# Attention layers: one program per engine for both halves, last block first, and the maxima split in four operations

## The reference

```python
x = x + _L0_xattn_ref(_layernorm(x), ctx_1024, mask_BxS2_bk0, ...)      # L0x: q and k normalised per head
x = x + _L0_attn_ref(_layernorm(x), ...)                                # L0a: self attention, j >= i
x = x + _L0_ffn_ref(_layernorm(x), ...)                                 # L0f: 8 experts, top 2
x = x + _L1_xattn_ref(_layernorm(x), ctx_1024, ctx_1024, mask, ...)     # L1x: mask per query and key
x = x + _L1_attn_ref(_layernorm(x), ...)                                # L1a: a window of 64 keys
x = x + _L1_ffn_ref(_layernorm(x), ...)                                 # L1f: 8 experts, top 2
```

## Time and profile before

| | |
|---|---|
| three runs | 1831.36, 1822.53, 1828.62 us (median 1828.62) |
| the profiled run | 1820.44 us, span of the core 1818.6 us |
| PE busy | 1631.3 us, 90% of the span |
| DVE busy | 1036.0 us, 57% |
| ACT busy | 530.2 us, 29% |
| POOL busy | 98.4 us, 5% |
| mean granted clock of PE | 0.949 of full |

### The profile page before, as it was taken

The page is one execution under the profiler, slowest core; times in us unless marked ns, Lnnn a source line. Parts: engine busy times, 40 slices in busy tenths (PEclk is TensorE's granted clock), DMA queues, the critical chain, the costliest instruction groups (busy, mean ns, idle before and its releaser), DMA issues. The chain is left out here.

```text
span 1818.6 us, 27921 instructions
## 1 busy us (share of the span) xinstructions
PE 1631.3 (90%) x9406; PEld 750.2 (41%) x9407; DVE 1036.0 (57%) x1695; ACT 530.2 (29%) x780; POOL 98.4 (5%) x82
## 2 busy tenths in 40 slices
PE   4899997999888979999999799997999788969997
PEld 1333333222233356665665233322222234467775
DVE  3577776999745541111111589996799734643223
ACT  1343423788412401111111111113588512300000
POOL 0100000200001010000001200002000001010001
PEclk9999988999989989999999799988999998979999
DMA  3424443311044749666661413315221020048996
GB/s 137 161 69 170 163 156 102 94 48 46 0 129 101 90 201 342 228 243 229 230 236 45 132 59 115 110 52 184 66 70 46 1 81 30 2 168 317 330 325 210
DMA packets 80244, 250.95 MB, mean 138 GB/s; under 512 B 7744, under 2 KB 25168, under 8 KB 60208
## 3 DMA queue, kind: packets, MB, share of 16 engines
q1 hardware_dynamic: 71568, 230.97, 38.1%
q10 hardware_dynamic: 6048, 10.69, 1.6%
q0 software_dynamic: 2560, 8.39, 1.4%
HBM read 222.50 MB, written 38.01 MB: 143 GB/s over the span
## 5 line engine op out<-in xcount | busy, mean ns | idle before, releaser
L1429 ACT ACTIVATE BIG<-banks 128x1024 f32<-128x1024 f32 (+5 forms) x320 | 282.1, 933 | 120.0 <-PE banks L1364 119.9
L993 DVE CUSTOM_DVE_ANT_0 BIG<-banks,MASK,MX 128x512 bf16<-128x512 f32 (+5 forms) x384 | 229.4, 656 | 68.2 <-issue 38.3
L1882 PE MATMUL banks<-KF,BIG 128*128 128x160 f32 (+1 forms) x1792 | 230.3, 289 | 5.0 <-DVE KF L1638 1.9
L1882 PEld LDWEIGHTS banks<-KF,BIG 128*128 128x128 f32 x1792 | 227.2, 191 | 17.2 <-issue 15.2
L654 PE MATMUL banks<-KF,XN 32*128 32x512 f32 (+4 forms) x1280 | 200.3, 633 | 16.6 <-DVE MX L993 7.7
L1904 PE MATMUL banks<-BIG,PB 128*128 128x512 f32 x448 | 202.8, 600 | 0.0
L1361 PE MATMUL banks<-XN,KF 32*128 32x512 f32 (+4 forms) x1280 | 173.3, 611 | 22.8 <-ACT BIG L1429 7.8
L1479 DVE TENSOR_TENSOR PB<-PB,BIG 128x2048 f32<-128x2048 f32 (+5 forms) x78 | 164.8, 2113 | 33.3 <-ACT BIG L1429 28.8
L986 DVE TENSOR_REDUCE MXW<-banks 128x2 f32<-128x1024 f32 x128 | 150.4, 1217 | 50.9 <-PE banks L665 49.8
L629 PE MATMUL banks<-WV,XNT 128*128 128x512 f32 x320 | 162.2, 628 | 0.0
L1331 PE MATMUL banks<-BIG,V 128*32 128x512 f32 (+4 forms) x1280 | 159.4, 568 | 3.2 <-ACT BIG L1429 2.8
(11 more groups left out here) (278 smaller groups left out, 1450.2 us busy)
## 6 DMA issues: line engine op xcount, KB each, us to landing
BIG<-in_L0f_w SPq DMA_DIRECT2D x64, 1024.0 KB, 4.7
BIG<-in_L1f_w SPq DMA_DIRECT2D x48, 1024.0 KB, 5.3
BIG<-in_mask_q SPq DMA_DIRECT2D x16, 1024.0 KB, 9.2
CT<-in_ctx SPq DMA_DIRECT2D x9, 1024.0 KB, 4.8
XNT<-in_ctx SPq DMA_DIRECT2D x8, 1024.0 KB, 5.9
k_saved<-KF SPq DMA_DIRECT2D x32, 256.0 KB, 2.6
v_saved<-V SPq DMA_DIRECT2D x32, 256.0 KB, 2.4
KF<-k_saved SPq DMA_DIRECT2D x32, 256.0 KB, 3.4
```

What stands on the lines that cost most here:

```text
L993: last = v.tensor_tensor_reduce(m.JUNK[:, 2 * half + e, k0:k1], pair[:, e, k0:k1], bias, 1.0, mx, ALU.add, ALU.max, mx)
L1429: a.activation(m.PE_[:, s % NP, 2 * half:2 * half + 2, q0:q1], m.pair[(2 * s + half) % 3][:, :, q0:q1], ACT.Exp).then_inc(exp_ready, 1)
L1882: last = t.matmul(out, W1[k][:, d, f * P:(f + 1) * P], XE[:, d, :], start=d == 0, stop=d == DC - 1)
```

## The change

`row_maxima` and `weighted_values` no longer open a program each. Both return the parts of the five engines, and `attention` opens one program in which an engine runs its part of the first half and then of the second. The semaphores of both halves are raised before it, with one barrier.

```diff
 def attention(nc, m, L, weights):
-    row_maxima(nc, m, L)
-    weighted_values(nc, m, L, weights)
+    A = row_maxima(nc, m, L)
+    first, second = A.parts, weighted_values(nc, m, L, weights, A)
+    raise_all(nc, m)
+    with nc.Block() as block:
+        @block.sync
+        def _(sp):
+            second.sync(sp, first.sync(sp))
...
```

```diff
-                with sp.If(i + 1 >= nb):
-                    for kb in range(KT_):
-                        keep_values(i, kb)
...
             if dyn:
-                load_mask(0)
-                for c in range(DC):
-                    load_keys(0, c)
-
-                for sem in m.past:
-                    wait_alone(sp, sem, nb * 16 + 16 + B)
+                if L.row_mask:
+                    wait_alone(sp, A.bias_ready, nb + A.B)
+                    load_mask(nb)
+                wait_alone(sp, A.context_loaded, nb * 16 + 16 + A.B)
+                wait_alone(sp, A.v_projected, nb * KT_ + A.B)
+            else:
+                sp.wait_ge(A.v_projected, KT_)
             O.load_output_weights(sp)
...
-                        load_keys(i + 1, c)
+                        load_keys(i, c)
```

```diff
-            v.tensor_scalar(R, m.MX[:, :], -1.0, None, ALU.mult).then_inc(steps_done, 1)
-            dve.wait_ge(cleared, 2)
-            k = 1
-            for j in range(3):
-                dve.wait_ge(steps_done, k)
-                v.tensor_copy(PART[:, :], R).then_inc(steps_done, 1)
-                dve.wait_ge(steps_done, k + 1)
-                v.tensor_copy(parts[:, :, j], PART[:, :]).then_inc(steps_done, 1)
-                v.tensor_tensor(R, R, PART[:, :], ALU.subtract).then_inc(steps_done, 1)
-                k += 3
...
+            dve.wait_ge(A.slots_zeroed, 2)
+            v.tensor_scalar(parts[:, :, 0], m.MX[:, :], -1.0, None, ALU.mult).then_inc(steps_done, 1)
+            dve.wait_ge(steps_done, 1)
+            v.scalar_tensor_tensor(R, m.MX[:, :], -1.0, parts[:, :, 0], ALU.mult, ALU.subtract).then_inc(steps_done, 1)
+            dve.wait_ge(steps_done, 2)
+            v.tensor_copy(parts[:, :, 1], R).then_inc(steps_done, 1)
+            dve.wait_ge(steps_done, 3)
+            v.tensor_tensor(parts[:, :, 2], R, parts[:, :, 1], ALU.subtract).then_inc(steps_done, 1)
...
+            pe.wait_ge(steps_done, 4)
+            pe.wait_ge(A.v_read, values_read)
             for c in range(DC):
                 for q in range(NQ):
                     at = (q * DC + c) * P
-                    last = nc.tensor.transpose(m.bank[c][:, q * P:(q + 1) * P], m.NMX[:, at:at + P], m.ident[:, :])
+                    last = t.matmul(m.bank[4 + c][:, q * P:(q + 1) * P], m.NMX[:, at:at + P], m.IDB[:, :], start=True, stop=True)
                 last.then_inc(transposed, 1)
...
+                if k == 0 and c < 2:
+                    M.ready(pe, 2 + c)
...
+                if k == 0:
+                    M.ready(pe, c)
+                elif (c, k) == (0, 1):
+                    M.ready(pe, 1)
...
             def body(i):
 
-                a.activation(m.WARM[:, :], m.MINUS1[0:1, :], ACT.Exp)
+                a.activation(m.WARM[:, 0:1], m.MINUS1[0:1, :], ACT.Exp)
...
+            a.activation(m.WARM[:, 1:2], m.MINUS1[0:1, :], ACT.Exp)
             M.scalar(act)
```

More of the change, by code:

```diff
@@ L136, in wait_alone, with to_raise @@
     eng.sem_inc(UNWAITED[0], 1)
-def raised(nc, m, loops, further={}):
+def to_raise(m, loops, further={}):
     fresh, m.fresh = m.fresh, []
@@ L1489, in _ @@
             if dyn:
-                for kb in range(KT_):
+                bias(0, 0)
+            if L.row_mask:
+                M.vector_flags(dve, nb)
+            M.vector_copies(dve)
+            if dyn:
+                for kb in range(1, KT_):
                     bias(0, kb)
+                dve.wait_ge(A.zeroed, DC + 1)
             over_blocks(dve, L, nb, body)
             O.vector(dve)
+    return Parts
 def attention(nc, m, L, weights):
-    row_maxima(nc, m, L)
-    weighted_values(nc, m, L, weights)
+    A = row_maxima(nc, m, L)
[5 more added lines that the diff above has]
+            second.sync(sp, first.sync(sp))
+        @block.tensor
+        def _(pe):
+            second.tensor(pe, first.tensor(pe))
+        @block.scalar
+        def _(act):
+            second.scalar(act, first.scalar(act))
+        @block.gpsimd
+        def _(pool):
+            second.gpsimd(pool, first.gpsimd(pool))
+        @block.vector
+        def _(dve):
+            second.vector(dve, first.vector(dve))
 def mixture(nc, m, tag, w1, w2, F, RS, probs, relu2, following=None, result=None):
```

192 lines of the change are left out of this document (107 added, 85 removed).

## The result

The changed kernel takes 1796.41 us, the median of four runs (1791.83 to 1800.98); the kernel before takes 1828.44 in the same comparison. The ratio is 0.9836, with a 95% interval of 0.9808 to 0.9863, so 32 us less (25 to 35 by the interval). The profiled run took 1800.98 us.

What follows compares the result with a forecast made beforehand. TensorE, busy for 90% of the 1818.6 us span, was taken as the bound; handover gains in four attention layers, 8.8 + 6.6 + 8.8 + 9.7, less 0.8 for semaphores, gave 33.1: 1828.6 - 33.1 = 1795.5 us, range 1784 to 1806.

## What to carry to other kernels

An idle gap without a releaser, on an engine that has just branched, is worth a look at the instruction queues: packets of them beside it are a hint that the engine waits for its code. They are not proof, since here they also came once without a gap; what showed it was that the gaps moved when the code was moved and went when the long jump went. Two long alternative bodies behind a flag can then cost more than a short branch in every step, and a change in the order of blocks can add such a gap without touching the code. And a loop's empty passes are paid where somebody waits for the engine to leave it: what stands behind the loop should be moved ahead of them only if nothing else behind the loop is then late.

## What the runs showed of the hardware

- A long jump of PE can stop it: for 3.4 to 4.9 us directly behind the jump, with two or three packets of 16 KB of its instruction queue between 1.4 us ahead of the gap and 2.5 us behind it, and for 4.4 to 6.3 us where the weights are being loaded. In no profile did the jump back from the form that stands second to the one that stands first do so. Which code is held at a time these runs don't settle: with some seven waits taken out of each form one gap vanished.
- Branches over four or eight matrix products, one or two in each step of 2.46 us, cost PE nothing measurable.
- Three passes of a loop in which an engine only compares and branches take DVE 2.2 us.
- Behind such a gap PE runs at half clock (unmasked steps of up to 4.31 us where 2.46 is usual). A gap of 3.4 to 4.1 us at the change from a masked to an unmasked block cost 4.7 to 6.3 in all.
